# Experts' attention: the split of the patches stands between sum and reciprocal, and its high half runs on ScalarE

## The reference

```
h  = (patches @ W + b, class token in front) * pos_embed      # 64 images x 65 tokens x 128
h  = h + attention(layernorm(h))                              # 8 heads of 16
h  = h + experts(layernorm(h))
experts: for each of 4 experts
    t = layernorm(relu(x @ w1 + b1) @ w2 + b2)                # 256 wide
    q, k, v = split(t @ w_in + b_in)                          # 16 heads of 16
    t = softmax(q k^T / 4) v @ w_out + b_out
    t = two LSTMs over t, gates, a decoder, layernorm
  outputs summed with softmax(x @ router)
```

## Time and profile before

| what | us |
|---|---|
| median of 3 runs | 3985.1 (3982.3 to 3990.77) |
| the profiled execution | 3987.37 |
| its span, first to last instruction | 3985.4 |
| granted TensorE clock, mean | 0.959 |
| first attention | about 268 to 390 of the span |
| experts' stage | about 485 to 1662 of the span |

### The profile page before, as it was taken

The page is one execution under the profiler, slowest core; times in us unless marked ns, Lnnn a source line. Parts: engine busy times, 40 slices in busy tenths (PEclk is TensorE's granted clock), DMA queues, the critical chain, the costliest instruction groups (busy, mean ns, idle before and its releaser), DMA issues. The chain is left out here.

```text
span 3985.4 us, 94491 instructions
## 1 busy us (share of the span) xinstructions
PE 3549.4 (89%) x35332; PEld 2154.8 (54%) x35332; DVE 2747.6 (69%) x4811; ACT 2115.4 (53%) x4188; POOL 1256.6 (32%) x1056
## 2 busy tenths in 40 slices
PE   6768778878878888899999999999999949999997
PEld 5644355555545545435555555555555537666665
DVE  7866688788688688766666666666666654555555
ACT  6857357657657657654444444444444455555554
POOL 0026467567567567520000000000000004444443
PEclk8989899989999999999999999999999969999999
DMA  9920100100100110231111111111111131111211
GB/s 175 176 53 17 43 16 0 44 16 0 44 16 1 44 65 1 86 122 45 50 45 50 45 50 45 50 45 50 45 50 45 45 113 51 56 43 54 56 56 31
DMA packets 391037, 203.23 MB, mean 51 GB/s; under 512 B 150861, under 2 KB 385106, under 8 KB 390234
## 3 DMA queue, kind: packets, MB, share of 16 engines
q1 hardware_dynamic: 390482, 201.03, 20.1%
q10 hardware_dynamic: 392, 0.03, 0.0%
HBM read 143.48 MB, written 57.51 MB: 50 GB/s over the span
## 5 line engine op out<-in xcount | busy, mean ns | idle before, releaser
L201 POOL MEMSET h_ident<- 128x128 f32 x1 | 0.2, 205 | 1444.2 <-POOLq L81 1444.2
L1866 ACT ACTIVATE l_gates<-l_gates 128x768 f32<-128x768 f32 x260 | 219.1, 843 | 349.4 <-DVE l_gates L1810 349.4
L1810 DVE SCALAR_TENSOR_TENSOR l_gates<-banks,l_unscale,l_bias 128x1024 f32<-128x1024 f32 x260 | 333.7, 1283 | 97.0 <-PE banks L1636 95.3
L665 POOL TENSOR_TENSOR ax_p<-ax_p,ax_ri 128x520 f32<-128x520 f32 (+1 forms) x256 | 320.2, 1252 | 220.6 <-DVE ax_ri L873 220.6
L1636 PE MATMUL banks<-l_w,l_xs 128*64 128x512 f16 x3120 | 361.9, 382 | 7.5 <-DVE l_xs L1723 6.6
L1636 PE MATMUL banks<-plot,l_xs 128*64 128x512 f16 x3120 | 359.9, 380 | 0.0
L2163 PE MATMUL banks<-h_mem,h_w 128*128 128x320 f16 x2496 | 357.6, 300 | 0.0
L1636 PE MATMUL banks<-l_w,out_t 128*64 128x512 f16 x3072 | 352.9, 379 | 1.7 <-DVE out_t L1729 1.7
L1636 PE MATMUL banks<-plot,out_t 128*64 128x512 f16 x3072 | 352.8, 379 | 0.0
L2458 ACT ACTIVATE h_work<-banks,h_bias,h_factor 128x320 f32<-128x320 f32 x312 | 192.4, 617 | 260.7 <-PE banks L2163 256.9
L1870 ACT ACTIVATE l_ig<-l_kept 128x256 f32<-128x256 f32 x260 | 108.2, 416 | 357.2 <-DVE l_kept L1827 355.3
(11 more groups left out here) (385 smaller groups left out, 7321.5 us busy)
## 6 DMA issues: line engine op xcount, KB each, us to landing
out_t<-x_scratch SPq DMA_DIRECT2D x130, 256.0 KB, 3.0
mem_scratch<-out_t SPq DMA_DIRECT2D x520, 64.0 KB, 2.0
h_mem<-mem_scratch SPq DMA_DIRECT2D x104, 320.0 KB, 3.6
image<-in_x_dram SPq DMA_DIRECT2D x132, 196.0 KB
x_scratch<-plot SPq DMA_DIRECT2D x4, 4160.0 KB, 16.3
ring<-in_x_dram SPq DMA_DIRECT2D x60, 196.0 KB
plot<-in_L_ffn_attn_in_w_dram SPq DMA_DIRECT2D x4, 768.0 KB, 4.6
h_scratch<-plot SPq DMA_DIRECT2D x1, 2080.0 KB, 6.5
```

Of the source, the lines that this page charges most:

```text
L665: pool.tensor_tensor(self.p[:, v, :, 0:k], self.p[:, v, :, 0:k], self.ri[:, v, :, 0:k].unsqueeze(3).broadcast_to([P, 2, k, SEQ]), ALU.mult ...
L1810: dve.scalar_tensor_tensor(out=gz.rearrange("p (n c) -> p n c", n=2), in0=ps[:, 2 * z:2 * z + 2, :], scalar=unscale[:, e:e + 1], in1=bias[ ...
L1866: act.activation(gates[:, z, 0:3 * D], gates[:, z, 0:3 * D], ACT.Sigmoid).then_inc(gated, 1)
```

## The change

A new method `act_split` does the high half on ScalarE, as an activation with a constant scale; `dve_split` keeps the low half and waits for the high one. In `act_run` it stands in s=0 behind the values' eviction and ahead of the copy of the turned probabilities. In `dve_run` the split is moved between the sum and the reciprocal of the image before. For the first unit of an expert ScalarE does the high half at step 9 of the weights stage. In the first attention `act_split` does nothing; its own `dve_split` is moved ahead of the reciprocal like the other, since `dve_run` is shared.

```diff
+    def act_split(self, act, unit, par):
+
+        act.wait_ge(self.x_moved, BASE + unit + 1)
+        act.activation(self.x[:, par, 0], self.x32[:, :, :, :], ACT.Copy, scale=NORMED).then_inc(self.x_high, 1)
+
     def dve_split(self, dve, src, unit, at, par, done):
 
         dve.wait_ge(self.x_moved, BASE + unit + 1)
         dve.wait_ge(self.v_done, BASE + done)
-        dve.tensor_scalar(self.x[:, par, 0], self.x32[:, :, :, :], NORMED, None, ALU.mult).then_inc(self.x_high, 1)
         dve.wait_ge(self.x_high, BASE + unit + 1)
         dve.scalar_tensor_tensor(out=self.x[:, par, 1], in0=self.x32[:, :, :, :], scalar=NORMED, in1=self.x[:, par, 0],
                                  op0=ALU.mult, op1=ALU.subtract).then_inc(self.x_low, 1)
@@ dve_run
                     dve.tensor_reduce(self.sm[:, v, :, 0:k], self.p[:, v, :, 0:k], AX.X, ALU.add).then_inc(self.summed, 1)
+                if s == 0 and self.unit_in(u, 1):
+                    self.dve_split(dve, src, unit + 1, at + 1, 1 - par, self.count(unit, u, 0))
+                if self.image_in(u, s, 1):
                     dve.wait_ge(self.summed, BASE + n(0))
                     dve.reciprocal(self.ri[:, v, :, 0:k], self.sm[:, v, :, 0:k]).then_inc(self.inverted, 1)
-                if s == 0 and self.unit_in(u, 1):
-                    self.dve_split(dve, src, unit + 1, at + 1, 1 - par, self.count(unit, u, 0))
@@ act_run
                     op.then_inc(self.v_kept, 1)
+                if s == 0 and self.unit_in(u, 1):
+                    self.act_split(act, unit + 1, 1 - par)
                 if self.image_in(u, s, self.TURN):
@@ experts_stage, scalar
+                def begin_first():
+
+                    act.wait_ge(att.v_done, BASE + e * att.COUNT)
+                    att.act_split(act, e * att.UNITS, 0)
+
+                laid_steps(body, {5: raise_weights, 9: begin_first,
+                                  WSTEPS + 1: lambda: att.act_keys(act, ps[:, 6, :], factor[:, 0:1], e * att.UNITS, 0)})
```

More of the change, by code:

```diff
@@ L1015, in dve_move, with act_split @@
     def dve_move(self, dve, src, unit, at):
+        pass
+    def act_split(self, act, unit, par):
         pass
@@ L1429, in raise_weights @@
                                    scale=w_scale[:, 0:1]).then_inc(w_high, 1)
-                laid_steps(body, {5: raise_weights, WSTEPS + 1: lambda: att.act_keys(act, ps[:, 6, :], factor[:, 0:1], e * att.UNITS, 0)})
+                def begin_first():
[3 more added lines that the diff above has]
+                                  WSTEPS + 1: lambda: att.act_keys(act, ps[:, 6, :], factor[:, 0:1], e * att.UNITS, 0)})
                 act.wait_ge(saved, BASE + e * 16)
```

## The result

The changed kernel takes 3946.95 us (median of 4, 3943.89 to 3949.25) against 3987.85 for the kernel before in the same runs: ratio 0.9899, 95% interval 0.9887 to 0.9911, 41 us less. The forecast was 3959 and 27 us less; the time lies inside the range of 3945 to 3985, close to its lower end. The direction and the mechanism held, the gain of a unit was mis-sized.

What follows compares the result with a forecast made beforehand. A chain through three engines, setting slot 2's value matmuls, bounds the kernel. 56 units at 0.46 give 25.8 us, first units 1.2, weights stage and first attention 0: 27 less, 3959; range 3945 to 3985.

Steps and rivals of the forecast that it cites:

- What bounds the loop: Experts' units: slot 2's value matmuls wait for key projections on the low half; VectorE then runs without idle gap.
- (a): Experts' units: high half leaves VectorE, 0.46 us per unit; ScalarE takes 0.62, covered by 1.6, no cost on the path.
- (b): Experts' units: low half, started before GpSimd's normalisation, falls from 1.43 to 0.69 us; bounds 0.69 and 1.43.
- The first unit's: First unit of each expert: low half meets the class mask, ends about 526.9 instead of 527.24; gain 0.3, 1.2 us altogether.
- The weights stage: VectorE waits for ScalarE about as long as it worked; 0 taken, bounds -1.4 and +0.9 us per expert.
- (c): Experts' units: late reciprocal delays normalisation and slot 2's mask, which ends last; value matmuls still 0.46 us earlier per unit.
- The other leg: Experts' units, slot 2: key projections on the completed x end at 665.20, before the mask's end at 665.51.
- PE follows a mask by 0.24: Experts' units: hand-over from GpSimd's mask to TensorE, read at 661.41 to 661.65, puts slot 2's value matmuls at 665.75.
- First attention: Only the order changes: VectorE wins 0.8, GpSimd loses 0.3, seven units; 0 taken, bounds -4 and +2 us.
- 1 (the low half keeps 1.43): Experts' units: its own length, or ScalarE stretches it; value matmuls 0.28 later, +15.7 us, about 4001; chance 9%.
- 2 (GpSimd doesn't bind): Experts' units: normalisation and mask end 0.55 earlier, projections bind, 1.01 per unit, -57 us, about 3930; chance 4%.
- 3 (no net change): Experts' units: new order costs at another slot what it wins, 0.4 us per unit suffices; about 3983; chance 8%.

Runs made afterwards that it cites:

- e4: Changed kernel with a second copy of ScalarE's high half into a spare tile ahead of the real one; 3948.95 us, ratio 0.9899 to the kernel before.
- e1: Kernel before with only the order changed: split, both halves on VectorE, ahead of the reciprocal in both attentions; 3973.65 us, ratio 0.9966.
- e6: Changed kernel with two further reciprocals into spare tiles ahead of the real one in slot 0 of the experts' units; 3949.14 us, ratio 0.9909.
- e2: Changed kernel with the order undone: ScalarE does the high half, reciprocal ahead of the low half again; 3947.77 us, ratio 0.9905 to the kernel before.
- e3: Changed kernel with GpSimd's normalisation of a unit's last image behind the mask of keys of slot 2, experts' attention only; 3934.49 us, ratio 0.9866.

## Why the prediction was right, and where its size was off

*What bounds the loop: right, with one error of reading.* The place (values of slot 2, held by projections on the low half) and the continuous run of VectorE behind it are as told. The text said that PE waits for the shift of the image just before; by the code it is the one before that, as the scores have two bank pairs. Nothing hung on it.

*(a) ScalarE's price: right.* 0.63 measured, 0.62 taken; 1.4 us of cover, 1.6 taken; e4 shows it off the path.

*(b) The low half: right.* 0.68 in all 14 units of each expert. The first unit's was not as good (1.03, held by the class mask until it ends), as worked out: 0.5 us gained there where the clock was alike, 0.3 taken. The forecast had no term for the clock, and this stretch is 1.4 to 2.1 us longer in both kernels wherever it is low, so the four first units together say nothing of this gain. The weights stage came out even, as taken: VectorE waits 1.56 us for ScalarE in place of 1.36 us of work.

*(c) GpSimd's chain: right in its order, and here is the term that was mis-sized.* The other leg, the projections, was right too: forecast to end 3.24 after the sum, measured 3.25 in that kind of unit. Steps from the sum's start, forecast and measured: low half 0.61 and 0.60, normalisation 1.50 and 1.47, mask 2.51 and 2.49, values 3.79 and 3.59. The first three hit within 0.03. The last step, "PE follows a mask by 0.24", did not: here it follows by 0.06, in e1 by 0.05, in e6 by 0.05. The 0.24 came from slot 1, where it still stands in the kernel after (mask to 639.96, values 640.20). So the gain is 0.66 instead of 0.46 at this place, and 0.64 by the period; 56 times the 0.18 missing is 10 us of the 14 by which the forecast fell short. I had one row of the hand-over and took it for another slot; its lower bound was zero, and with it the unit's gain would have had the ends 0.46 and 0.70.

*First attention: a little better.* 1.1 us gained where 0 was taken, bounds -4 and +2. It is the order: e2, without it, has 99.83 us there, as before, and e1, with nothing else, 98.66.

*Rivals.* 1 (the low half keeps 1.43) fell with the 0.68 of the changed kernel, and with e1 and e2. Its clause on ScalarE fell too: the exponential (640.24, 0.75) lies beside the start of the low half at 640.73, and that takes 0.68. 2 (GpSimd doesn't bind) fell with e3. 3 (no net change) fell with the time.

What the forecast did not see is that either half of the change does part of the work: the order alone gives 15 us, ScalarE's part alone 41, both together 41. Once the high half is off VectorE, the low half starts ahead of the normalisation by itself in all but one unit of an expert, and the new order adds nothing that the medians can tell; the traces have 0.02 us of a period and 1.1 us of the first attention for it.

## What to carry to other kernels

Where VectorE and GpSimd both work from SBUF to SBUF, look at the starts and not only at the durations: an instruction at twice its free length (1.43 for 0.68 here) may be waiting for the other engine, and 0.1 us of head start can turn that round. When an instruction is made late on purpose, follow it through the queue of the engine that it releases: behind the normalisation stood a mask that the critical matmuls needed, and putting that mask first gave as much again as a third of the change. Take a hand-over time from the very slot it is used for.

## What the runs showed of the hardware

- The low half, 128x512 with two SBUF inputs, took 0.68 to 0.69 us free, 1.43 when it started 0.35 into a normalisation of GpSimd, 1.34 where it started 0.27 into one, 0.75 to 0.80 where the end of a mask reached into it (e3), and 1.03 to 1.06 in the first unit and the weights stage of the changed kernel. GpSimd's normalisation took 1.06 free and 1.53 when it started 0.09 us after the low half.
- The hand-over from GpSimd's mask to TensorE's matmuls was 0.05 to 0.06 us in slot 2 and 0.24 in slot 1, in every kernel whose PE waited for the mask there. In e1 PE stood idle before either (0.49 and 0.98; in the other kind of unit 0.72 to 0.73 before slot 2 and 0.59 to 0.63 before slot 1), so neither idleness nor its length explains it. The cause stays open.
- The seam between two experts varies by itself. In e3, one kernel and one execution, the stretch from the last split of an expert to the next expert's first took 89.98 and 85.30 us with the same instructions on each engine; the granted TensorE clock (the column behind GpSimd's) was 0.92 and 0.98, a mix of its two levels, 1.2 and 2.4 GHz. Table by stretches in e3:

```profile
1000.51:1090.49 89.98, 78.56 (x589) 46.57 (x586) 58.54 (x83) 50.07 (x102) 39.95 (x31) 0.92 0.18 49
1295.31:1380.61 85.30, 74.39 (x589) 44.58 (x586) 58.48 (x83) 50.04 (x102) 39.89 (x31) 0.98 0.19 52
```

  From the last maximum of an expert to the first of the next, before and after have 90.52, 90.95, 90.17 and 87.66, 89.52, 89.97 us, and the nine traces of this study lie between 87.4 and 91.3. That is enough to carry the 6 us that the units, the first attention and the first units leave unexplained, so this remainder is left open.
